# Probability transposes one step later, and one score matmul over both halves of k for a head's first query tile

## The chip, the cores and the metric

The kernel runs on one NeuronCore of a Trainium2 chip. The metric is the device time of one execution in microseconds (us). TensorE (PE) multiplies, VectorE (DVE) and ScalarE (ACT) do elementwise work and reductions, GpSimd (POOL) does slower elementwise work, SyncE (SP) issues the DMAs. Each engine runs its own queue of instructions in order, and engines wait for one another by semaphores.

## The reference

Four sequences of 512 tokens, width 1024, go through attention with 16 heads of 64 and then through a mixture of low-rank experts. What matters here is the attention:

```python
q = apply_rotary(norm(x) @ Wq)          # also k; v without rotary
logits = einsum('bhqd,bhkd->bhqk', q, k)
logits = where(causal, logits, -1e9) / sqrt(64)
attn = softmax(logits)
out = einsum('bhqk,bhkd->bhqd', attn, v) @ Wo
x = x + norm(out)
x = x + norm(expert_mixture(norm(x)))
```

## The kernel before

Every float32 operand of a matmul is split into a high part in a format that TensorE takes at full rate (`fp32r`) and a low part, the remainder. A projection is three products, high by high, low by high and high by low.

**Units and slots.** The attention is cut into 32 units. Unit u is one pair of heads of one sequence. A slot is the program stretch in which unit u is projected; it has 8 steps, s = 0 to 7. `slot(pair, b, half, ahead)` is written out for each engine, and `run_slots` calls it in the same order for all: some slots are written out, most lie in loops of two slots, b = 0 and b = 1. Slot number u is odd where b is 1. In the slots with `ahead` (u = 2 to 9) a further tile of x is normalised, transposed and stored for the second half. `closing` slots 32 and 33 have no projection.

**The eight score tiles.** A unit has 2 heads with 4 query tiles of 128 each, so q = 0 to 7; tile i = q % 4 of a head sees 128 x (i + 1) keys because of the causal mask. Because `trailing(u, s, 1)` shifts by one step, tile q of unit u - 1 is worked on in step s = q + 1 of slot u (q = 7 in step 0 of slot u + 1). For each tile:

- TensorE, `scores`: two matmuls into the score bank, stationary q_hl (the rows of one head's q high, the other 64 rows its low part), moving k_hh (k high in both halves of the partitions) and then k_lo (k low in the head's own half, zeros in the other). Both have 128 x (i + 1) columns and add into the same columns.
- VectorE, `negate` (L1053): adds the causal mask to the scores, scales by a negative factor and takes the running minimum, which gives prob (not yet exponentiated) and nmax.
- ScalarE, `exponent` (L740): the exponential with its sum.
- VectorE, `invert` (L1063): the reciprocal of the sum.
- GpSimd, `divide` (L595): prob times that reciprocal.
- TensorE, `turn_probs` (L1499), two steps later: `trailing(u, s, 3)`: i + 1 transposes of 128x128 into a pT bank.
- ScalarE, `pt_high` (L751), copies the high part out, then VectorE, `pt_low` (L1071), subtracts it for the low part. Both are in the step of the transposes.

**The rest of a slot.** `project` is 72 matmuls of 512 columns, 9 per step in three thirds; the scores stand behind the first third, the transposes behind the second. `attend` (L1517 to L1520) multiplies the transposed probabilities by v: head 0 at s = 0, head 1 at s = 4, of unit u - 2. Its result has two halves: ScalarE's `o_lower` (L784) copies the lower half out (s = 1 and s = 5) and VectorE's `o_add` (L1105) adds it to the upper half (s = 1 and s = 6, between `negate` and `invert`). VectorE has `rotate` (L1080, the rotary product, s = 3 and 6, also between `negate` and `invert`), `q_low` (L1085, s = 4 and 5, after `pt_low`), `v_low` (L1096, s = 2), and `k_low` (L1091 and L1092, a subtraction that gives k_lo and a copy within k_hh; head 0 at s = 7 after `pt_low`, head 1 at s = 0 of the next slot). ScalarE has `v_raw` (s = 0), `v_high` (s = 2), `q_high` (s = 3), `k_high` (s = 6). The first scores of a unit wait for `k_low` of head 0.

**Weights.** For each pair of slots, in the slots with b = 1, GpSimd's `w_pairs` (L606, L607) stands at s = 2 and 5 and `w_low` (L613) at s = 4 and 7, behind that step's `divide`, and ScalarE's `w_high` (L733) at s = 4 and 6. The third weight's `w_high` and `w_low` are in the slot with b = 0 at s = 0 and s = 1.

Each engine's order is the order in which its `slot` is written: for ScalarE `exponent`, `v_raw` or `o_lower`, `v_high`, `pt_high`, the others; for VectorE `negate`, `rotate`, `o_add`, `invert`, `v_low`, `pt_low`, the others. With `ahead`, `k_low` of head 0 stands before `invert`, and VectorE also has statistics (L990, L991, L996) at s = 4 and their scale at s = 6.

After the units come sixteen token tiles of output projection and experts, which the change doesn't touch.

Of the kernel before, what the change touches and what calls it, by code (L numbers as in the profile page):

```python
# [19 lines left out]
F32R = mybir.dt.float32r  # L20
# [43 lines left out]
HOLD_AT = (4, 7)  # L64
X_BANKS = (4, 5, 6, 7, 2, 3)


def sandwich_kernel(nc, x, wqkv, wo, ar, bt, br, cos, sin, scratch, out):
    with ExitStack() as ctx:
# [3 lines left out]
        def sem(name):  # L73
            return ctx.enter_context(nc.semaphore(name))
# [64 lines left out]
        k_hh = sb(sB, "k_hh", [P, 2, 2, SEQ], F32R)  # L139
        k_lo = sb(sB, "k_lo", [P, 2, 2, SEQ], F32R)  # L140
# [14 lines left out]
        o_sum = sb(sB, "o_sum", [DH, 2, SEQ])  # L155

# [67 lines left out]
        neg_done = sem("neg_done")  # L224
        exp_done = sem("exp_done")
# [470 lines left out]
        def _(act):  # L696
# [47 lines left out]
            def pt_high(u, s):  # L744
                a, q, g = trailing(u, s, 3)
                if real(a):
                    i, h = q % QT, q // QT
                    act.wait_ge(t_done, g + 1)
                    if late(a, 1):
                        act.wait_ge(pv_done, 2 * a + h - 1)  # L750
                    act.activation(pT_hi[:, h, 0:i + 1, P * i:P * i + P],  # L751
                                   pt_ps[q % 2][:, 0:P * (i + 1)].rearrange("p (j t) -> p j t", j=i + 1),
                                   ACT.Copy).then_inc(pt_hi_done, 1)
# [46 lines left out]
            def slot(pair, b, half, ahead=False):  # L800
# [6 lines left out]
                for s in range(STEPS):  # L807
# [3 lines left out]
                    if s == 1 and real(u - 2):  # L811
                        o_lower(u - 2, 0)
                    if s == 5 and real(u - 2) and not (isinstance(u, int) and u > UNITS):
                        o_lower(u - 2, 1)
# [173 lines left out]
        def _(dve):  # L988
# [56 lines left out]
            def negate(u, s):  # L1045
                a, q, g = trailing(u, s, 1)
                if real(a):
                    n = P * (q % QT + 1)
                    dve.wait_ge(s_done, g + 1)
                    if late(g, 4):  # L1050
                        dve.wait_ge(t_done, g - 3)
                    dve.sem_inc(gate_dve, 1)
                    dve.tensor_tensor_reduce(prob[:, q % 4, 0:n], sc_ps[q % 2][:, 0:n], mask[:, SEQ - n:SEQ],  # L1053
                                             -SOFT, 3e38, ALU.add, ALU.min, nmax[:, q % 4:q % 4 + 1]
                                             ).then_inc(neg_done, 1)
# [9 lines left out]
            def pt_low(u, s):  # L1065
                a, q, g = trailing(u, s, 3)
# [57 lines left out]
            def slot(pair, b, half, ahead=False):  # L1124
# [4 lines left out]
                for s in range(STEPS):  # L1129
# [7 lines left out]
                    if s == 1 and real(u - 2) and not closing:  # L1137
                        o_add(u - 2, 0)
                    if s == 6 and real(u - 2) and not (closing and u > UNITS):
                        o_add(u - 2, 1)  # L1140
# [11 lines left out]
                    if closing and s == 1 and real(u - 2):  # L1152
                        o_add(u - 2, 0)
                    if real(u):
                        if s in (4, 5):
                            q_low(u, b, s - 4)
                        if s == 7 and not leads:
                            k_low(u, b, 0)
# [240 lines left out]
        def _(pe):  # L1399
# [76 lines left out]
            def scores(u, s, b):  # L1476
                a, q, g = trailing(u, s, 1)
                if real(a):
# [5 lines left out]
                    if late(g, 2):  # L1484
                        pe.wait_ge(neg_done, g - 1)
                    qc, kc = slice(P * i, P * i + P), slice(0, P * i + P)
                    products(sc_ps[q % 2][:, kc], [(q_hl[:, ab, h, qc], k_hh[:, ab, h, kc]),
                                                   (q_hl[:, ab, h, qc], k_lo[:, ab, h, kc])], True, True
                             ).then_inc(s_done, 1)

            def turn_probs(u, s):
                a, q, g = trailing(u, s, 3)
# [58 lines left out]
            def slot(pair, b, half, ahead=False):  # L1551
                u = 2 * pair + b + UPH * half
                n = pair + PAIRS * half
                for s in range(STEPS):
# [13 lines left out]
                    if s == 0:  # L1568
                        attend(u - 2, b, 0)
                    if s == (3 if isinstance(u, int) and u == UNITS + 1 else 4):  # L1570
                        attend(u - 2, b, 1)
# [191 lines left out]
```

## Time and profile before

| | |
|---|---|
| median of 3 runs | 1069.91 us (1069.79 to 1070.48) |
| the profiled execution | 1069.58 us |
| its span, first to last instruction | 1067.8 us |
| TensorE busy | 1049.9 us |
| VectorE, ScalarE, GpSimd busy | 756.9, 591.3, 439.4 us |
| mean granted TensorE clock | 0.998 |
| attention units | to about 820 us |

The profile is one execution. TensorE's matmuls overlap in its pipeline, so its busy time says that something was always in flight, not that no start was late; late starts are read from the distances between starts. An idle time with a releaser tells which instruction of which engine ended it. A row's second number is the duration; the distance between two starts is the cost in a queue.

### The profile page before, as it was taken

Reading aid. Unit: us, or ns where it says so; the run is one execution under the profiler, and the core shown is the slowest. Engines: PE = TensorE matmul, PEld = TensorE weight load, DVE = VectorE, ACT = ScalarE, POOL = GpSimd, SP = SyncE. Lnnn points to the kernel's source line nnn. Section 1 sums busy time; section 2 is a strip of 40 time slices with the busy share of each in tenths; the row PEclk is TensorE's granted clock in tenths of the full one; section 3 lists DMA queues with packets and bytes.
Section 4 is the critical chain, followed back from the end, with each engine's and each line's share of the span. In section 5 each row is a group of like instructions: output and inputs, shape, how many; then the busy total and the mean of one; then the engine's idle time right before and its main releaser. Section 6 shows DMA issues by size and latency. Waiting matters only on the chain.

```text
span 1067.8 us, 20069 instructions
## 1 busy us (share of the span) xinstructions
PE 1049.9 (98%) x5559; PEld 871.3 (82%) x5559; DVE 756.9 (71%) x2138; ACT 591.3 (55%) x1390; POOL 439.4 (41%) x422
## 2 busy tenths in 40 slices
PE   7999999999999999999999999999999999999996
PEld 6888888888888888888888888888877888888884
DVE  8777777776666666666666666666766877777777
ACT  7556666666555665565555655555576333333334
POOL 4153443435353635444452625344457232333221
PEclk9999999999999999999999999999999999999999
DMA  7022324241311256021111112020333323322311
GB/s 280 36 84 70 128 69 128 74 129 55 104 51 34 95 182 227 10 71 33 52 49 31 52 29 69 10 69 17 87 132 93 108 88 107 118 99 87 109 61 60
DMA packets 58663, 90.36 MB, mean 85 GB/s; under 512 B 3568, under 2 KB 36336, under 8 KB 58608
## 3 DMA queue, kind: packets, MB, share of 16 engines
q1 hardware_dynamic: 58464, 89.44, 25.9%
q8 instruction: 25, 0.41, 0.2%
q14 instruction: 30, 0.25, 0.1%
q10 hardware_dynamic: 144, 0.26, 0.1%
HBM read 64.52 MB, written 25.17 MB: 84 GB/s over the span
## 4 chain that ended last, share of the span: by engine, by line
PE 90%; DVE 3%; issue 2%; ACT 2%; POOL 0%; DVEq 0%; ACTq 0%; POOLq 0%
PE bank L1472 46%; PE bank L1403 25%; PE bank L1499 6%; PE bank L1518 3%; PE bank L1517 3%; PE bank L1633 2%; PE bank L1610 1%; PE bank L1445 1%; PE bank L1634 1%; PE bank L1520 1%; PE bank L1433 1%; ACT prob L740 1%; DVE prob L1053 0%; DVE k_hh L1092 0%; PE bank L1415 0%
## 5 line engine op out<-in xcount | busy, mean ns | idle before, releaser
L595 POOL TENSOR_SCALAR prob<-prob,rinv 128x128 f32<-128x128 f32 (+3 forms) x256 | 150.5, 588 | 436.8 <-DVE rinv L1063 436.8
L1472 PE MATMUL bank<-big_hi,w_hi 128*128 128x512 f32 (+1 forms) x776 | 329.4, 424 | 0.3 <-DVE big_lo L1034 0.3
L740 ACT ACTIVATE prob<-prob,nmax 128x128 f32<-128x128 f32 (+3 forms) x256 | 144.0, 562 | 304.3 <-DVE nmax L1053 302.7
L1472 PE MATMUL bank<-big_hi,w_lo 128*128 128x512 f32 (+1 forms) x776 | 304.5, 392 | 0.0
L1472 PE MATMUL bank<-big_lo,w_hi 128*128 128x512 f32 (+1 forms) x776 | 302.1, 389 | 0.0
L1472 PEld LDWEIGHTS bank<-big_hi,w_lo 128*128 128x128 f32 x776 | 145.6, 188 | 33.2
L1071 DVE TENSOR_TENSOR pT_lo<-bank,pT_hi 128x128 fp32r<-128x128 f32 (+3 forms) x256 | 123.7, 483 | 56.0 <-ACT pT_hi L751 53.3
L1472 PEld LDWEIGHTS bank<-big_hi,w_hi 128*128 128x128 f32 x776 | 146.6, 189 | 16.5 <-issue 0.4
L1472 PEld LDWEIGHTS bank<-big_lo,w_hi 128*128 128x128 f32 x776 | 147.1, 190 | 11.6
L1063 DVE RECIPROCAL rinv<-rsum 128x1 f32<-128x1 f32 x256 | 40.8, 159 | 129.3 <-ACT prob L740 128.9
L1053 DVE CUSTOM_DVE_ANT_0 prob<-bank,mask 128x128 f32<-128x128 f32 (+3 forms) x256 | 124.1, 485 | 9.2 <-PE bank L1403 5.1
L1499 PE MATMUL bank<-ident,prob 128*128 128x128 f32 x640 | 112.0, 273 | 1.5 <-POOL prob L595 1.0
L751 ACT ACTIVATE pT_hi<-bank 128x128 fp32r<-128x128 f32 (+3 forms) x256 | 108.8, 425 | 2.1 <-PE bank L1499 0.5
L1499 PEld LDWEIGHTS bank<-ident,prob 128*128 128x128 f32 x640 | 82.9, 141 | 32.5 <-POOL prob L595 6.0
L674 POOL TENSOR_TENSOR res<-res,x 128x1024 f32<-128x1024 f32 x14 | 33.4, 2389 | 146.1 <-ACT res L705 146.1
L613 POOL TENSOR_TENSOR w_lo<-w_sum,w_hi 128x1024 fp32r<-128x1024 f32 x32 | 83.0, 2593 | 8.0 <-ACT w_hi L733 7.7
L1403 PE MATMUL bank<-k_lo,q_hl 128*128 128x128 f32 (+3 forms) x256 | 82.2, 321 | 0.0
L1403 PE MATMUL bank<-k_hh,q_hl 128*128 128x128 f32 (+3 forms) x256 | 80.7, 315 | 0.5 <-DVE k_hh L1092 0.5
L1403 PE MATMUL bank<-big_hi,w_hi 128*128 128x512 f32 x192 | 79.5, 414 | 0.0
L1403 PE MATMUL bank<-big_lo,w_hi 128*128 128x512 f32 x192 | 75.2, 391 | 0.0
L1403 PE MATMUL bank<-big_hi,w_lo 128*128 128x512 f32 x192 | 75.0, 391 | 0.0
L1105 DVE TENSOR_TENSOR o_sum<-bank,o_low 64x512 f32<-64x512 f32 x64 | 43.3, 677 | 37.5 <-ACT o_low L784 37.5
(146 smaller groups left out, 1927.7 us busy)
## 6 DMA issues: line engine op xcount, KB each, us to landing
w_raw<-in_wqkv SPq DMA_DIRECT2D x48, 512.0 KB, 4.4
attention_out<-o_sum SPq DMA_DIRECT2D x64, 128.0 KB, 2.3
w_raw<-attention_out SPq DMA_DIRECT2D x16, 512.0 KB, 4.8
land<-in_x SPq DMA_DIRECT2D x16, 512.0 KB, 3.7
out<-res SPq DMA_DIRECT2D x14, 512.0 KB, 2.6
xin<-in_x SPq DMA_DIRECT2D x12, 512.0 KB, 5.7
xT_hold_hi<-xin SPq DMA_DIRECT2D x8, 512.0 KB, 3.6
xT_hold_lo<-xn SPq DMA_DIRECT2D x8, 512.0 KB, 5.4
```

The source lines that it names most:

```text
L595: pool.tensor_scalar(p, p, rinv[:, q % 4:q % 4 + 1], 1.0, ALU.mult, ALU.mult).then_inc(prob_done, 1)
L613: pool.tensor_tensor(w_lo[:, m, :], src, w_hi[:, m, :].bitcast(F32), ALU.subtract).then_inc(w_lo_done[m], 1)
L674: pool.tensor_tensor(res[:, i, :], res[:, i, :], x1[:, i, :], ALU.add).then_inc(res_done, 1)
L740: act.activation(prob[:, q % 4, 0:n], prob[:, q % 4, 0:n], ACT.Exp, scale=-1.0, bias=nmax[:, q % 4:q % 4 + 1], accum_out=rsum[:, q % 4:q % ...
L751: act.activation(pT_hi[:, h, 0:i + 1, P * i:P * i + P], pt_ps[q % 2][:, 0:P * (i + 1)].rearrange("p (j t) -> p j t", j=i + 1), ACT.Copy).t ...
L1053: dve.tensor_tensor_reduce(prob[:, q % 4, 0:n], sc_ps[q % 2][:, 0:n], mask[:, SEQ - n:SEQ], -SOFT, 3e38, ALU.add, ALU.min, nmax[:, q % 4:q ...
L1063: dve.reciprocal(rinv[:, q % 4:q % 4 + 1], rsum[:, q % 4:q % 4 + 1]).then_inc(inv_done, 1)
L1071: dve.tensor_tensor(pT_lo[at], pt_ps[q % 2][:, 0:P * (i + 1)].rearrange("p (j t) -> p j t", j=i + 1), pT_hi[at].bitcast(F32), ALU.subtract ...
L1105: dve.tensor_tensor(o_sum[:, h, :], o_ps[0:DH, :], o_low[:, :], ALU.add).then_inc(osum_done, 1)
L1403: mm = pe.matmul(dst, lhsT, rhs, start=first and n == 0, stop=last and n == len(terms) - 1)
L1472: done = pe.matmul(grp_ps[(b + k) % 2][:, cols], w, xt[:, cols], start=at == 0, stop=at == GROUP_MM - 1)
L1499: last = pe.transpose(pt_ps[q % 2][:, P * j:P * j + P], prob[:, q % 4, P * j:P * j + P], ident[:, :])
```

## The change

`TURN_LAG = 4` takes the place of the 3 in `turn_probs`, `pt_high` and `pt_low`: transposes and what follows them come one step later (for step s the tile is now q = s - 4 modulo 8 instead of s - 3). `attend` moves from s = 0 and 4 to s = 1 and 5 (in the last slot from 3 to 4), `o_lower` from s = 1 and 5 to 2 and 6, and `o_add` from s = 1 and 6 to s = 2 and 6, where it now stands behind `pt_low` and not before `invert`.

For a head's first query tile (i = 0) the two score matmuls of 128 columns become one of 256: k_hh and k_lo are now the halves of one tensor k_all, the moving operand is [2 x 128] columns of it, and the two products lie side by side in the score bank. VectorE adds the second to the mask first, waits for that, and uses the result in place of the mask.

```diff
+TURN_LAG = 4
-        k_hh = sb(sB, "k_hh", [P, 2, 2, SEQ], F32R)
-        k_lo = sb(sB, "k_lo", [P, 2, 2, SEQ], F32R)
+        k_all = sb(sB, "k_all", [P, 2, 2, 2, SEQ], F32R)
+        k_hh, k_lo = k_all[:, 0, :, :, :], k_all[:, 1, :, :, :]
...
             def pt_high(u, s):
-                a, q, g = trailing(u, s, 3)
+                a, q, g = trailing(u, s, TURN_LAG)
...
-                    if s == 1 and real(u - 2):
+                    if s == 2 and real(u - 2):
                         o_lower(u - 2, 0)
-                    if s == 5 and real(u - 2) and not (isinstance(u, int) and u > UNITS):
+                    if s == 6 and real(u - 2) and not (isinstance(u, int) and u > UNITS):
                         o_lower(u - 2, 1)
...
+                    added = mask[:, SEQ - n:SEQ]
+                    if q % QT == 0:
+                        added = low_masked[:, :]
+                        dve.tensor_tensor(added, sc_ps[0][:, P:2 * P], mask[:, SEQ - P:SEQ], ALU.add).then_inc(low_added, 1)
+                        dve.wait_ge(low_added, 2 * a + q // QT + 1)
+                        dve.sem_inc(gate_dve, 1)
-                    dve.tensor_tensor_reduce(prob[:, q % 4, 0:n], sc_ps[q % 2][:, 0:n], mask[:, SEQ - n:SEQ],
+                    dve.tensor_tensor_reduce(prob[:, q % 4, 0:n], sc_ps[q % 2][:, 0:n], added,
...
             def pt_low(u, s):
-                a, q, g = trailing(u, s, 3)
+                a, q, g = trailing(u, s, TURN_LAG)
...
-                    if s == 1 and real(u - 2) and not closing:
-                        o_add(u - 2, 0)
-                    if s == 6 and real(u - 2) and not (closing and u > UNITS):
-                        o_add(u - 2, 1)
...
-                    if closing and s == 1 and real(u - 2):
+                    if s == 2 and real(u - 2):
                         o_add(u - 2, 0)
+                    if s == 6 and real(u - 2) and not (closing and u > UNITS):
+                        o_add(u - 2, 1)
...
+                    if i == 0:
+                        pe.matmul(sc_ps[0][:, 0:2 * P].rearrange("p (a n) -> p a n", a=2), q_hl[:, ab, h, qc],
+                                  k_all[:, :, ab, h, kc], start=True, stop=True).then_inc(s_done, 1)
...
             def turn_probs(u, s):
-                a, q, g = trailing(u, s, 3)
+                a, q, g = trailing(u, s, TURN_LAG)
...
-                    if s == 0:
+                    if s == 1:
                         attend(u - 2, b, 0)
-                    if s == (3 if isinstance(u, int) and u == UNITS + 1 else 4):
+                    if s == (4 if isinstance(u, int) and u == UNITS + 1 else 5):
                         attend(u - 2, b, 1)
```

## Rows read from the trace of the kernel before

**Rows 1.** The page: engine, busy us, share of the span, number of instructions.
```profile
PE 1049.9 (98%) x5559; PEld 871.3 (82%) x5559; DVE 756.9 (71%) x2138; ACT 591.3 (55%) x1390; POOL 439.4 (41%) x422
```

**Rows 2.** TensorE's waits, whole span: line, releaser, us in total, times, longest.
```profile
PEld bank L1499 <- POOL prob L595: 6.0, 12, 1.4
...
PE bank L1403 <- DVE k_hh L1092: 0.5, 1, 0.5
```

**Rows 3.** Waits of VectorE and of ScalarE between 100 and 780 us.
```profile
DVE rinv L1063 <- ACT prob L740: 112.5, 154, 1.7
...
DVE prob L1053 <- PE bank L1403: 0.2, 1, 0.2
...
ACT prob L740 <- DVE nmax L1053: 267.5, 169, 4.7
```

**Rows 4.** VectorE's timeline, negations of two slots: start us, duration us, engine, line.
```profile
583.51 0.29 DVE L1053 CUSTOM_DVE_ANT_0 prob<-bank,mask 128x128 f32<-128x128 f32 x1
...
608.53 0.29 DVE L1053 CUSTOM_DVE_ANT_0 prob<-bank,mask 128x128 f32<-128x128 f32 x1
...
611.24 0.41 DVE L1053 CUSTOM_DVE_ANT_0 prob<-bank,mask 128x256 f32<-128x256 f32 x1
...
614.01 0.55 DVE L1053 CUSTOM_DVE_ANT_0 prob<-bank,mask 128x384 f32<-128x384 f32 x1
...
615.78 0.69 DVE L1053 CUSTOM_DVE_ANT_0 prob<-bank,mask 128x512 f32<-128x512 f32 x1
...
622.46 0.42 DVE L1053 CUSTOM_DVE_ANT_0 prob<-bank,mask 128x256 f32<-128x256 f32 x1
...
624.67 0.54 DVE L1053 CUSTOM_DVE_ANT_0 prob<-bank,mask 128x384 f32<-128x384 f32 x1
...
627.81 0.69 DVE L1053 CUSTOM_DVE_ANT_0 prob<-bank,mask 128x512 f32<-128x512 f32 x1
...
631.76 0.29 DVE L1053 CUSTOM_DVE_ANT_0 prob<-bank,mask 128x128 f32<-128x128 f32 x1
```

**Rows 5.** TensorE's timeline around a first-tile and a second-tile score pair.
```profile
508.65 0.22 PE L1403 MATMUL bank<-k_hh,q_hl 128*128 128x128 f32 x1
...
509.34 0.40 PE L1472 MATMUL bank<-big_hi,w_lo 128*128 128x512 f32 x1
...
511.85 0.28 PE L1403 MATMUL bank<-k_lo,q_hl 128*128 128x256 f32 x1
...
512.43 0.39 PE L1472 MATMUL bank<-big_hi,w_lo 128*128 128x512 f32 x1
```

**Rows 6.** Instructions by line and form: busy us, mean ns, idle before.
```profile
L1071 DVE TENSOR_TENSOR pT_lo<-bank,pT_hi 128x512 fp32r<-128x512 f32 x64 | 43.2, 676 | 3.1 <-ACT pT_hi L751 3.1
...
L1071 DVE TENSOR_TENSOR pT_lo<-bank,pT_hi 128x128 fp32r<-128x128 f32 x64 | 18.6, 290 | 0.0
...
L751 ACT ACTIVATE pT_hi<-bank 128x512 fp32r<-128x512 f32 x64 | 37.3, 584 | 0.5 <-PE bank L1499 0.5
...
L751 ACT ACTIVATE pT_hi<-bank 128x128 fp32r<-128x128 f32 x64 | 16.4, 257 | 0.0
```

**Rows 7.** VectorE's timeline: an instruction that waits for the one before it.
```profile
152.69 0.21 DVE L996 BATCH_NORM_AGGREGATE mv<-stats 128x2 f32<-128x12 f32 x1 [0.15 <-DVE stats L991]
```

**Rows 8.** ScalarE's timeline: the o_low copy.
```profile
620.01 0.60 ACT L784 ACTIVATE o_low<-bank 64x512 f32<-64x512 f32 x1
```

**Rows 9.** Timelines of VectorE and GpSimd around 312 us.
```profile
311.28 0.87 DVE L1091 TENSOR_TENSOR k_lo<-rot,k_hh 64x512 fp32r<-64x512 f32 x1 [0.16 <-issue]
312.17 2.57 DVE L1092 CAST k_hh<-k_hh 64x512 fp32r<-64x512 f32 x1
...
311.58 2.87 POOL L613 TENSOR_TENSOR w_lo<-w_sum,w_hi 128x1024 fp32r<-128x1024 f32 x1
```

**Rows 10.** VectorE's timeline: first negation of unit 1 and of unit 8.
```profile
67.61 0.29 DVE L1053 CUSTOM_DVE_ANT_0 prob<-bank,mask 128x128 f32<-128x128 f32 x1
...
244.39 0.29 DVE L1053 CUSTOM_DVE_ANT_0 prob<-bank,mask 128x128 f32<-128x128 f32 x1
```

More of the change, by code:

```diff
@@ L155, in sandwich_kernel @@
         o_sum = sb(sB, "o_sum", [DH, 2, SEQ])
+        low_masked = sb(sB, "low_masked", [P, P])
         hold_hi = xin[:, 1, :].rearrange("p (c t) -> p c t", c=KC)
@@ L224, in sandwich_kernel @@
         neg_done = sem("neg_done")
+        low_added = sem("low_added")
         exp_done = sem("exp_done")
@@ L1486, in scores @@
                     qc, kc = slice(P * i, P * i + P), slice(0, P * i + P)
-                    products(sc_ps[q % 2][:, kc], [(q_hl[:, ab, h, qc], k_hh[:, ab, h, kc]),
-                                                   (q_hl[:, ab, h, qc], k_lo[:, ab, h, kc])], True, True
-                             ).then_inc(s_done, 1)
+                    if i == 0:
+                        pe.matmul(sc_ps[0][:, 0:2 * P].rearrange("p (a n) -> p a n", a=2), q_hl[:, ab, h, qc],
+                                  k_all[:, :, ab, h, kc], start=True, stop=True).then_inc(s_done, 1)
+                    else:
+                        products(sc_ps[q % 2][:, kc], [(q_hl[:, ab, h, qc], k_hh[:, ab, h, kc]),
+                                                       (q_hl[:, ab, h, qc], k_lo[:, ab, h, kc])], True, True
+                                 ).then_inc(s_done, 1)
             def turn_probs(u, s):
-                a, q, g = trailing(u, s, 3)
+                a, q, g = trailing(u, s, TURN_LAG)
                 if real(a):
```

## Prediction

> **What bounds the kernel now.** I read the busy shares first. TensorE is busy 98% of the span and VectorE 71% [rows 1]. That page invites the sum "TensorE work removed is time removed". So I read next what TensorE waits for: its weight loads for the probability transposes stood 6.0 us behind GpSimd's division in the whole span, 12 times, 1.4 us at most [rows 2]. Almost nothing is lost on TensorE.
>
> Then I asked whether the others have room, from the waits of VectorE and ScalarE between 100 and 780 us, where the attention units run. VectorE waited 112.5 us for ScalarE's exponential, ScalarE 267.5 us for VectorE's negation, and VectorE only once, for 0.2 us, for scores of TensorE [rows 3]. So these two engines wait for each other and not for TensorE: they are a loop of their own. Its period is in VectorE's timeline. The first negation of a unit (128x128) starts at 583.51, 608.53 and 631.76 us [rows 4]: 25.02 us for a unit in an odd slot, 23.23 in an even one, 48.25 for the pair, 24.13 per unit. In the steady part I find these lengths repeated to 0.02 us in most units, which a queue fed by TensorE wouldn't do. TensorE's own stream has a period of 24.16. The kernel has two chains of one length, and only one looks busy. This is the main reading: whatever lengthens the VectorE-ScalarE loop by more than a few hundredths of a us per unit appears in the time.
>
> The eight intervals between negations in the even slot are 2.71, 2.77, 1.77 for the tiles q = 0, 1, 2, then 6.68 for q = 3 and 4 together, 2.21, 3.14 and 3.95 for q = 5, 6, 7 [rows 4].
>
> **TensorE's part.** From the start of a first-tile score pair to the start of the third matmul behind it are 0.69 us (508.65 to 509.34); from a single 256-column score matmul to the same place 0.58 (511.85 to 512.43) [rows 5]. The change turns the first into the second: 0.11 x 64 heads = 7.0 us off TensorE, about 0.22 per unit, period 23.94. If the two-part operand streamed badly, the nearest bound on the other side is the pair as it is, 0; neither end matters while the other loop is longer. The later transposes give the division one more step, some 3 us, so the waits of [rows 2] go; what they cost TensorE's own timeline I take as at most 1.4. At the end of attention the last transposes are now directly in front of the last `attend`, with no matmuls between: the 512-column ScalarE copy and VectorE subtraction, 0.58 + 0.68 us [rows 6], with hand-over some 1.4, become a wait there. These two cancel.
>
> **The added VectorE instruction.** The low-part addition is 128x128 from PSUM and SBUF, the form and size of the negation, 0.29 us [rows 4]. The negation has to wait for it on its own engine with a gate increment between, as the statistics' aggregation does: 0.15 us idle [rows 7]. 0.45 per head, 0.9 per unit. Queued behind it are the negation, so ScalarE's exponential, and everything behind both. Bounds: 0.29 (wait free) to 0.6 (wait twice as long). The 29% idle of VectorE doesn't hide it, since that idle is its waiting inside the loop.
>
> **What moves inside the loop.** Each interval is reworked from the one of before (even slot, which is free of weight work), following which of the two engines comes last.
> q = 0: the o_low copy (0.60 us [rows 8]) and the o_sum addition leave it. What remains is the bare pattern of q = 2 (1.77), 0.5 less for a third as many columns in negation and exponential, 0.2 more for a 256- instead of a 128-column turn: 1.48. Plus 0.45: 1.93 against 2.71, -0.78.
> q = 1: o_low now stands before v_high on ScalarE (+0.60 and its issue), o_sum behind pT_lo on VectorE (+0.61), and the turn has 384 columns, not 512 (-0.13): 3.97 against 2.77, +1.20.
> q = 2: its turn was 128 columns and is 512: +0.33 on ScalarE and +0.39 on VectorE [rows 6], less 0.06 that the reciprocal hides: 2.42, +0.65.
> q = 3 and 4: o_low leaves (-0.7), narrower turns (-0.5), the addition comes (+0.45): 5.95 against 6.68, -0.73.
> q = 5: before, o_sum ran while ScalarE worked and cost nothing. Now o_low delays the copy pT_hi by 0.6, and o_sum (0.6) stands behind pT_lo; the turn is 384 instead of 512 columns (-0.2): 3.29, +1.08.
> q = 6: turn of 512 instead of 128 columns in front of k_low, +0.71, less 0.2 for a division that no longer meets k_low: 3.64, +0.50.
> q = 7: 128 columns instead of 256: 3.65, -0.30.
> Sum 24.85 against 23.23: **+1.62 us in an even slot**. So the order costs 0.7 to 0.8 beside the addition's 0.9: the two o_low/o_sum steps no longer stand where the other engine's work covered them, and the wide turns now meet the steps in which VectorE has rotate and k_low.
>
> **The odd slot** has the weight work. The same differences give 25.02 + 1.62 = 26.64, less 0.7 because the second q_low now loses less to GpSimd's weight sums, less 0.1 at q = 6: 25.8, +0.8. But k_low comes 0.71 later. In this profile k_lo starts at 311.28 and GpSimd's w_lo (128x1024) at 311.58, and the copy k_hh then took 2.57 us instead of 0.42, ending 0.29 after w_lo [rows 9]: VectorE's SBUF-only copy stood still for GpSimd's instruction. It happened fully once, at 312 us, because k_lo is usually just ahead. With k_lo 0.71 later, w_lo is in front by about 0.4 in every odd slot: k_lo then waits for the rest of w_lo, some 2.0 us, less what the division's meeting cost: 27.4, **+2.4 us in an odd slot**. The Trainium skill (SBUF — State Buffer, Who interferes with whom) says that a VectorE instruction with two SBUF inputs, or in a two-port mode, contends with GpSimd, and that whoever issues first holds the pair for the whole instruction. By that rule the wait is the rest of w_lo, as this row shows; if the port were shared by halves, the odd slot would cost some 1 us less. The same section says that an instruction with one SBUF input doesn't contend, so by it the new addition is free of this.
>
> **The sum.** Steady units 9 to 29, 11 even and 10 odd: 11 x 1.62 + 10 x 2.40 = 41.8, less 2.2 for the one meeting already paid at 312 us: 39.6. Units 1 to 7, in which later x tiles are prepared as well, took 244.39 - 67.61 = 176.8 us [rows 10]; the same differences apply, save that q = 3 is held by statistics and division (0 instead of -0.17) and that k_low there precedes the turn (no lock): 188.8, +12.0. Unit 8 +1.5, unit 0 +0.7. The last two units and the closing slots, which have o_low and o_sum too: +3, bounds 0 to 6. TensorE's slack before the scores of each unit (under 1 us) is used up once: -0.8. Together +56.0. The profiled execution took 1069.6 us (span 1067.8), 0.3 below the median of the runs: 1069.6 + 56.0 = 1125.6, and I forecast 1125. The part behind 830 us isn't touched. On TensorE's 7.0 us nothing is gained: it waits at the first scores of a unit for k_low.
>
> **Rivals.**
> (1) The order costs what I say, but w_lo and k_lo don't meet, because GpSimd or ScalarE falls into another phase: odd slots 25.8 instead of 27.4, so 10 x 1.6 = 16 less, 1109. For it: the meeting needs 0.4 us of phase. Against: GpSimd starts w_lo at a fixed distance from the reciprocal.
> (2) **Faster**: VectorE's and ScalarE's idle absorbs the additions, and TensorE's stream sets the period. Place: the unit loop; price: -7.0 and -1.4 of lost waits, +1.4 at the end: 1062.6. It decides if the loop's pair period stays below 2 x 23.94 = 47.9 us. For it: 29% idle VectorE. Against: the period is 48.25 already, with no wait for TensorE in [rows 3].
> (3) The loop lengthens by the additions only, since moving o_low and o_sum off q = 0 and q = 4 repays itself: 0.9 x 30 = 27, less the slack of 0.8: 1096.
> (4) Worse: more VectorE copies meet GpSimd, or TensorE's granted clock falls behind waits of 2 to 4 us per pair of units (it is 0.998 over the span now): above 1138.
> (5) The merged matmul isn't cheaper at all. It would change nothing while (2) is false, and is counted in the forecast.
>
> **How the numbers follow.** Forecast 0.58, covering 1115 to 1136 through the bounds of the addition and of the closing slots; (1) 0.22, 1100 to 1115; (3) 0.07, 1085 to 1100; (2) 0.07; (4) 0.05; 0.01 for no change. The range that holds 8 in 10 with part of (3) is 1092 to 1138. About 0.2% is what a measurement of this kernel can tell from no change: faster 0.07, same 0.02, slower 0.91.
>
> **What would show it.** In the changed profile: the eight intervals (1.93, 3.97, 2.42, 5.95, 3.29, 3.64, 3.65) from VectorE's timeline; pair period 52.3; q = 6 interval near 6.0 in odd slots with a k_lo of 2 us or more; TensorE waiting for k_hh at the first scores of a unit, some 30 times, where it is now once, for 0.5 us [rows 2]; no more wait for the division; VectorE still with no wait for TensorE. It would be wrong if VectorE showed waits for scores in the steady part, or if the pair period were below 48.

## The result, and the profile after

The changed kernel takes **1144.53 us** (median of 4 runs, 1143.57 to 1145.21) against 1069.99 (1069.79 to 1070.48): ratio 1.0695, 95% interval 1.0677 to 1.0714. The profiled execution took 1143.57 us, span 1141.7. So it is slower, as forecast, but by 74 us where 56 were forecast, and above the range's upper end of 1138.

The page of the changed kernel, busy us of each engine and the granted TensorE clock in tenths over 40 slices:

```profile
PE 1074.2 (94%) x5495; PEld 878.2 (77%) x5495; DVE 790.3 (69%) x2202; ACT 591.2 (52%) x1390; POOL 428.4 (38%) x422
...
PEclk9999999999999899999898999999899999999999
```

TensorE has 64 instructions fewer than in [rows 1] and yet 24.3 us more busy time. No removed matmul can explain that; the row of clocks shows TensorE working at a lower clock for a part of the time: four slices fall to 8, and the mean over the span is 0.975 where it was 0.998.

Waits between 100 and 840 us of the changed kernel (line, releaser, us in total, times, longest):

```profile
ACT prob L743 <- DVE nmax L1062: 329.3, 210, 4.6
DVE rinv L1072 <- ACT prob L743: 118.9, 182, 1.2
PE bank L1495 <- DVE k_all L1101: 41.0, 17, 3.6
...
DVE prob L1062 <- PE bank L1410: 12.2, 10, 2.0
DVE prob L1062 <- DVE low_masked L1059: 11.1, 55, 0.6
```

Against [rows 2, 3]: TensorE now waits 41.0 us for the copy k_hh, 17 times, up to 3.6 us at a time, where it waited 0.5 once. VectorE waits for ScalarE and ScalarE for VectorE still, and longer. The last two lines are the added wait behind the low-part addition, and one that I had said would not appear: VectorE waiting ten times, up to 2.0 us, for a score matmul.

**One odd slot of the changed kernel**, negations in VectorE's timeline (start us, duration us), with what ended an idle time in brackets, and the first two of the even slot behind it:

```profile
630.67 0.29 DVE L1062 CUSTOM_DVE_ANT_0 prob<-bank,low_masked 128x128 f32<-128x128 f32 x1 [0.19 <-DVE low_masked L1059]
632.14 0.42 DVE L1062 CUSTOM_DVE_ANT_0 prob<-bank,mask 128x256 f32<-128x256 f32 x1
634.49 0.69 DVE L1105 TENSOR_TENSOR v_hl<-bank,v_hl 128x512 fp32r<-128x512 f32 x1 [1.08 <-ACT v_hl L779]
...
636.16 0.54 DVE L1062 CUSTOM_DVE_ANT_0 prob<-bank,mask 128x384 f32<-128x384 f32 x1
638.58 0.68 DVE L1062 CUSTOM_DVE_ANT_0 prob<-bank,mask 128x512 f32<-128x512 f32 x1
...
642.26 0.29 DVE L1062 CUSTOM_DVE_ANT_0 prob<-bank,low_masked 128x128 f32<-128x128 f32 x1 [0.19 <-DVE low_masked L1059]
644.61 0.42 DVE L1062 CUSTOM_DVE_ANT_0 prob<-bank,mask 128x256 f32<-128x256 f32 x1
...
647.92 0.54 DVE L1062 CUSTOM_DVE_ANT_0 prob<-bank,mask 128x384 f32<-128x384 f32 x1
...
653.97 0.69 DVE L1062 CUSTOM_DVE_ANT_0 prob<-bank,mask 128x512 f32<-128x512 f32 x1
...
658.17 0.29 DVE L1062 CUSTOM_DVE_ANT_0 prob<-bank,low_masked 128x128 f32<-128x128 f32 x1 [0.19 <-DVE low_masked L1059]
661.72 0.42 DVE L1062 CUSTOM_DVE_ANT_0 prob<-bank,mask 128x256 f32<-128x256 f32 x1 [1.99 <-PE bank L1410]
```

The slot lasts 658.17 - 630.67 = 27.50 us. Its intervals are 1.47, 4.02, 2.42, then 3.68 + 2.35 = 6.03, 3.31, 6.05, 4.20. The prediction counted the addition and its wait (0.48 from start to start) with q = 0, here they lie at the end of q = 7; counted as there: 1.95, 4.02, 2.42, 6.03, 3.31, 6.05, 3.72 against 1.93, 3.97, 2.42, 5.95, 3.29, near 6.0, 3.65. **The reworked intervals held to 0.1 us.** Only the last line doesn't fit: q = 0 of the even slot took 3.55 instead of 1.47, and VectorE waited 1.99 of them for scores.

**What happens there** is in the slot two units earlier, at 596 us: GpSimd's w_lo and VectorE's k_lo and k_hh of the changed kernel,

```profile
596.14 2.34 POOL L616 TENSOR_TENSOR w_lo<-w_sum,w_hi 128x1024 fp32r<-128x1024 f32 x1
...
596.31 2.71 DVE L1100 TENSOR_TENSOR k_all<-rot,k_all 64x512 fp32r<-64x512 f32 x1
599.03 0.42 DVE L1101 CAST k_all<-k_all 64x512 fp32r<-64x512 f32 x1
...
602.04 0.69 DVE L1100 TENSOR_TENSOR k_all<-rot,k_all 64x512 fp32r<-64x512 f32 x1
```

TensorE's timeline behind it,

```profile
599.59 0.57 PE L1495 MATMUL bank<-k_all,q_hl 128*128 128x256 f32 x1 [3.29 <-DVE k_all L1101]
599.96 0.63 PE L1479 MATMUL bank<-big_hi,w_hi 128*128 128x512 f32 x1
600.39 0.63 PE L1479 MATMUL bank<-big_lo,w_hi 128*128 128x512 f32 x1
...
606.73 0.39 PE L1479 MATMUL bank<-big_hi,w_hi 128*128 128x512 f32 x1
606.96 0.40 PE L1479 MATMUL bank<-big_lo,w_hi 128*128 128x512 f32 x1
```

and TensorE in stretches of 3 us (stretch, its length, busy us and instructions, granted clock, DMA share, GB/s):

```profile
596.00:599.00 3.00, 0.30 (x2) 0.98 0.84 337
599.00:602.00 3.00, 2.41 (x7) 0.50 0.01 3
602.00:605.00 3.00, 3.00 (x11) 0.50 0.00 0
605.00:608.00 3.00, 3.00 (x19) 0.89 0.00 0
608.00:611.00 3.00, 3.00 (x17) 1.00 0.00 0
```

k_lo starts 0.17 us behind w_lo and takes 2.71 instead of 0.69, ending 0.54 after w_lo. TensorE stands still for 3.29 us until k_hh is there. Then its granted clock is 0.50, the 1.2 GHz level, over two stretches, although from 602 on it works without a gap; 512-column matmuls start 0.43 us apart (599.96, 600.39) instead of 0.23 (606.73, 606.96). In those six microseconds 18 matmul records stand where the next six have 36. So the scores of q = 1 come late, and VectorE and ScalarE, which set the time, wait for them.

**The account** goes by the first negation of a unit in the changed kernel (units 1, 8, 9 and 30; unit 0 starts at 42.85, and in the kernel before units 0, 9 and 30 at 42.35, 269.06 and 777.13):

```profile
70.20 0.29 DVE L1062 CUSTOM_DVE_ANT_0 prob<-bank,low_masked 128x128 f32<-128x128 f32 x1 [0.19 <-DVE low_masked L1059]
...
256.73 0.29 DVE L1062 CUSTOM_DVE_ANT_0 prob<-bank,low_masked 128x128 f32<-128x128 f32 x1 [0.19 <-DVE low_masked L1059]
...
282.57 0.29 DVE L1062 CUSTOM_DVE_ANT_0 prob<-bank,low_masked 128x128 f32<-128x128 f32 x1 [0.56 <-DVE low_masked L1059]
...
845.76 0.29 DVE L1062 CUSTOM_DVE_ANT_0 prob<-bank,low_masked 128x128 f32<-128x128 f32 x1 [0.19 <-DVE low_masked L1059]
```

| stretch | before, us | after, us | measured | forecast |
|---|---|---|---|---|
| to the first negation | 42.35 | 42.85 | +0.5 | 0 |
| unit 0 | 25.26 | 27.35 | +2.1 | +0.7 |
| units 1 to 7 | 176.78 | 186.53 | +9.8 | +12.0 |
| unit 8 | 24.67 | 25.84 | +1.2 | +1.5 |
| units 9 to 29 | 508.07 | 563.19 | +55.1 | +39.6 |
| unit 30 and all behind it | 290.67 | 295.94 | +5.3 | +3.0 |
| TensorE's slack | | | | -0.8 |
| span | 1067.8 | 1141.7 | +73.9 | +56.0 |

The clock's part can be read here. Of the +55.1, the lengthened q = 0 of the even slots is 13.0: it is 1.47 where nothing disturbs it, and in the ten even slots from unit 11 to 29 it took 2.15, 3.32, 1.92, 2.28, 3.40, 3.50, 3.55, 2.05, 2.28 and 3.28. The other 42.1 is the order, the additions and the meeting of k_lo with w_lo. Unit 1, in the stretch before, lost 0.8 in the same way (q = 0 is 2.28 there, and 1.47 in e3 below).

### The profile page after: what moved, and what is told of

Its sections match the earlier page's. It is cut to its first block, busy times and chain, and to the rows that moved or that the text cites. A ratio compares the mean times of both kernels' runs of the same rounds, so it can differ in the third digit from the quotient of the medians.

```text
span 1141.7 us, 20114 instructions
## 1 busy us (share of the span) xinstructions
PE 1074.2 (94%) x5495; PEld 878.2 (77%) x5495; DVE 790.3 (69%) x2202; ACT 591.2 (52%) x1390; POOL 428.4 (38%) x422
## 4 chain that ended last, share of the span: by engine, by line
PE 60%; issue 14%; DVE 11%; ACT 10%; DVEq 1%; ACTq 1%; POOL 0%; POOLq 0%
PE bank L1479 26%; PE bank L1410 19%; PE bank L1510 4%; ACT pT_hi L754 3%; PE bank L1529 3%; ACT prob L743 3%; DVE prob L1062 2%; PE bank L1528 2%; ACT o_low L787 2%; PE bank L1644 2%; DVE k_all L1100 1%; PE bank L1621 1%; PE bank L1495 1%; PE bank L1452 1%; ACT k_all L769 1%
## 5 line engine op out<-in xcount | busy, mean ns | idle before, releaser
L1479 PE MATMUL bank<-big_hi,w_lo 128*128 128x512 f32 (+1 forms) x776 | 308.4, 397 | 0.0
L1479 PE MATMUL bank<-big_lo,w_hi 128*128 128x512 f32 (+1 forms) x776 | 307.4, 396 | 0.0
L1479 PEld LDWEIGHTS bank<-big_hi,w_lo 128*128 128x128 f32 x776 | 148.6, 191 | 34.5
L1479 PEld LDWEIGHTS bank<-big_hi,w_hi 128*128 128x128 f32 x776 | 149.7, 193 | 17.4 <-issue 0.6
L1479 PEld LDWEIGHTS bank<-big_lo,w_hi 128*128 128x128 f32 x776 | 150.4, 194 | 11.5
L1062 DVE CUSTOM_DVE_ANT_0 prob<-bank,mask 128x256 f32<-128x256 f32 (+2 forms) x192 | 105.7, 551 | 17.4 <-PE bank L1410 15.2
L1410 PE MATMUL bank<-k_all,q_hl 128*128 128x256 f32 (+2 forms) x384 | 99.9, 341 | 0.0
L616 POOL TENSOR_TENSOR w_lo<-w_sum,w_hi 128x1024 fp32r<-128x1024 f32 x32 | 79.0, 2470 | 6.7 <-ACT w_hi L736 6.0
L1410 PEld LDWEIGHTS bank<-k_all,q_hl 128*128 128x128 f32 x384 | 69.7, 188 | 13.8
L1529 PE MATMUL bank<-pT_lo,v_hl 128*64 128x512 f32 (+3 forms) x256 | 67.0, 329 | 0.0
```

The lines of the kernel that those rows point to most:

```text
L616: pool.tensor_tensor(w_lo[:, m, :], src, w_hi[:, m, :].bitcast(F32), ALU.subtract).then_inc(w_lo_done[m], 1)
L1410: mm = pe.matmul(dst, lhsT, rhs, start=first and n == 0, stop=last and n == len(terms) - 1)
L1479: done = pe.matmul(grp_ps[(b + k) % 2][:, cols], w, xt[:, cols], start=at == 0, stop=at == GROUP_MM - 1)
L1529: pe.matmul(o_ps[0:DH, cols], v_hl[:, b, j, h, 0:DH], pT_lo[:, h, j, cols], start=False, stop=False)
```

## The experiments

The theory: VectorE and ScalarE in turn set the time; the additions, the order of the later steps and the meeting of k_lo with w_lo lengthen their loop; and the wait of TensorE behind that meeting drops its clock. Each part is taken alone, then mended.

**e2: the merged matmul and the addition alone**, everything else where it was.

```
 AHEAD = EARLY // 2
-TURN_LAG = 4
+TURN_LAG = 3
...
-                    if s == 2 and real(u - 2):
+                    if s == 1 and real(u - 2):
                         o_lower(u - 2, 0)
...
-                    if s == 1:
+                    if s == 0:
                         attend(u - 2, b, 0)
```

(o_add, the second o_lower and the second attend go back to their steps of before in the same way.)

> The merged score matmul with the addition on VectorE, but transposes, attend, o_lower and o_add where they were before. Loop theory: intervals of before plus 0.45 at q = 0 and q = 4, pair period 48.25 + 1.8 = 50.05 us, 1.75 over TensorE's 48.3: 10.5 pairs x 1.75 = 18, the units with x tiles 7 x 0.9 = 6, the last ones 1 to 2: 1095 us, q = 6 in odd slots near 4.0 (k_lo still ahead of GpSimd's w_lo), and no cut of TensorE's clock. Rival (VectorE's idle hides the addition and TensorE's 7 us are gained): 1063.

Measured: 1095.66 us (1095.53 to 1096.04), ratio 1.0242 (1.0225 to 1.026). Its waits between 100 and 840 us, and the first negation of three successive units:

```profile
PE bank L1512 <- POOL prob L598: 9.1, 22, 1.7
```

```profile
602.40 0.29 DVE L1062 CUSTOM_DVE_ANT_0 prob<-bank,low_masked 128x128 f32<-128x128 f32 x1 [0.19 <-DVE low_masked L1059]
...
627.90 0.29 DVE L1062 CUSTOM_DVE_ANT_0 prob<-bank,low_masked 128x128 f32<-128x128 f32 x1 [0.19 <-DVE low_masked L1059]
...
652.10 0.29 DVE L1062 CUSTOM_DVE_ANT_0 prob<-bank,low_masked 128x128 f32<-128x128 f32 x1 [0.19 <-DVE low_masked L1059]
```

The pair of units lasts 49.70 us instead of 48.25 [rows 4]. 64 matmuls fewer, and 25.8 us more, of 64 x 0.48 = 30.7 us added on VectorE. The idle 29% of VectorE hides none of it in an even slot, which takes 24.20 us instead of 23.23. An odd slot takes 25.50 instead of 25.02: there the q = 4 interval falls from 4.20 to 3.71 with its addition in place at q = 3, since the second q_low, now later, takes 1.10 us beside GpSimd's weight sums instead of 1.58. TensorE isn't what sets the time; its shorter work shows as new waits for GpSimd's division. This settles the main reading against rival (2). Over the whole kernel the new addition costs 0.40 per head (25.8 / 64).

**e1: the order alone**, without the merged matmul and the addition.

```
-                    if q % QT == 0:
-                        added = low_masked[:, :]
-                        dve.tensor_tensor(added, sc_ps[0][:, P:2 * P], mask[:, SEQ - P:SEQ], ALU.add).then_inc(low_added, 1)
-                        dve.wait_ge(low_added, 2 * a + q // QT + 1)
-                        dve.sem_inc(gate_dve, 1)
...
-                    if i == 0:
-                        pe.matmul(sc_ps[0][:, 0:2 * P].rearrange("p (a n) -> p a n", a=2), q_hl[:, ab, h, qc],
-                                  k_all[:, :, ab, h, kc], start=True, stop=True).then_inc(s_done, 1)
-                    else:
...
```

> The later transposes with the moved attend, o_lower and o_add, but the scores of a first query tile as before: two matmuls, no addition on VectorE. The loop theory (VectorE and ScalarE are a loop of their own that sets the time of a unit): against the changed kernel each unit loses two additions of 0.45 us, so 0.9, in all about 28 of its 1144.5 us, and some more where TensorE's wait becomes short enough that its clock isn't cut: 1101 to 1116 us, with intervals between negations as in the changed kernel (4.02, 2.42, 3.68 to the next, and so on), and q = 6 in odd slots still near 6.0. The rival, that the added instruction is the whole loss and the new order costs nothing, gives the time of before, 1070, or a little less.

Measured: 1110.54 us (1107.76 to 1111.44), ratio 1.0375 (1.0358 to 1.0392). The q = 6 interval of odd slots is 6.06 to 6.13, so the meeting with w_lo comes from the order and needs no addition. TensorE's waits for k_hh are shorter than in the changed kernel:

```profile
PE bank L1405 <- DVE k_all L1096: 26.5, 13, 2.9
```

2.9 us at most, not 3.6, and the mean granted clock is 0.992: the drop shows in a few slots only (q = 0 took 2.89 at unit 1, 4.09 at unit 11 and 2.72 at unit 13, else 1.5 to 1.7). e1 and e2 together give 40.6 + 25.8 = 66.4 of the 74.5 that the whole change costs; the other 8 us come only with both. The clock can account for them: the three long intervals of e1 hold 5.3 us of excess, those of the changed kernel 13.8 (both with unit 1).

**e3: the changed kernel without the meeting.** GpSimd holds back the second w_lo until k_lo and k_hh of the slot are done.

```
                         if s in (4, 7):
+                            if s == 7:
+                                pool.wait_ge(qk_lo_done, 4 * u + 3)
                             w_low(s // 7, n + 1)
```

> The changed kernel, but GpSimd starts the w_low of step 7 only once k_low of head 0 is done. If w_lo holds up k_lo in each odd slot and the wait of TensorE that comes of it (up to 3.6 us) cuts its clock, both go: q = 6 in odd slots from 6.05 to 3.9 to 4.4, the interval at q = 0 in even slots from 1.47 to 3.55 back to 1.47 everywhere, granted clock near 1.0: about 18 + 12 to 15 off, 1110 to 1115 us. If the meeting isn't the cause, the time stays at 1144. If it is, but the clock has another cause, 1126.

Measured: 1110.75 us (1110.35 to 1111.36), ratio 1.0384 (1.0367 to 1.0402), 34 us below the changed kernel. Its k_lo of both heads and its w_lo in an odd slot, TensorE's waits for k_hh, and the span with the clock:

```profile
630.18 0.67 DVE L1102 TENSOR_TENSOR k_all<-rot,k_all 64x512 fp32r<-64x512 f32 x1
630.87 0.42 DVE L1103 CAST k_all<-k_all 64x512 fp32r<-64x512 f32 x1
...
633.88 1.12 DVE L1102 TENSOR_TENSOR k_all<-rot,k_all 64x512 fp32r<-64x512 f32 x1
```

```profile
631.37 2.42 POOL L616 TENSOR_TENSOR w_lo<-w_sum,w_hi 128x1024 fp32r<-128x1024 f32 x1 [1.33 <-DVE k_all L1103]
```

```profile
PE bank L1497 <- DVE k_all L1103: 31.7, 27, 1.6
```

```profile
core 0: 1108.6 us, clock 0.999
```

k_lo of head 0 takes 0.67 again, the q = 6 interval of odd slots is 4.01, q = 0 is 1.47 in every unit from 1 to 30, and VectorE has no wait for scores. w_lo waits 1.33 us, and this isn't quite free: it moves the division behind it, and k_lo of head 1 (at 633.88) then takes 1.12 us where an even slot's takes 0.69, so the q = 7 interval of odd slots is 4.63 instead of 4.20. The wait of TensorE is still there 27 times, but 1.6 us at most, and the clock stays at its upper level. So one cause, the meeting, brings both the longer odd slot and the lost clock: about 20 us and 14 us, as the next run divides them.

**e4: the clock by itself.** The meeting stays; TensorE is kept at work in front of the first scores of an even slot by 12 matmuls into a bank that the scores overwrite.

```
+                    if s == 1 and b == 0 and real(u) and not ahead and not (isinstance(u, int) and u == 0):
+                        pe.wait_ge(neg_done, STEPS * (u - 1) - 1)
+                        for _ in range(12):
+                            pe.matmul(sc_ps[0][:, :], w_hi[:, 0, 0:P], xT_hi[:, b, 0, :], start=True, stop=True)
                     scores(u, s, b)
```

> The changed kernel with 12 more matmuls of 512 columns on TensorE ahead of the first scores of a unit in even slots (from unit 9 on), where it waits for k_hh up to 3.6 us; their results are overwritten by the scores. They take 12 x 0.23 = 2.8 us of that wait. If the cut clock is what stretches q = 0 in even slots (1.47 to 3.55), it stays at 1.5 to 2.0 there, the granted clock is near 1.0 and VectorE no longer waits for scores, while q = 6 in odd slots stays 6.05: about 10 to 14 us less, 1131 to 1135. If the stretch has another cause (a transfer, the order of transposes), the time stays at 1144 or grows.

Measured: 1130.84 us (1130.52 to 1131.79), ratio 1.0572 (1.0554 to 1.0589): **13.7 us less although TensorE does more**. TensorE around the added matmuls, and the stretches behind them:

```profile
643.66 2.90 PE L1578 MATMUL bank<-big_hi,w_hi 128*128 128x512 f32 x12
647.12 0.39 PE L1495 MATMUL bank<-k_all,q_hl 128*128 128x256 f32 x1 [0.56 <-DVE k_all L1101]
```

```profile
645.00:648.00 3.00, 2.44 (x11) 1.00 0.42 172
648.00:651.00 3.00, 3.00 (x19) 1.00 0.00 0
```

The scores still start when k_hh is there, so the meeting is untouched (q = 6 of odd slots 6.15, 0.1 more than without the added matmuls), but the granted clock is 1.00 behind it, the scores of q = 1 are in time, and q = 0 of even slots is 1.47. The 13.7 us agree with the 13.0 read from the intervals. What remains of e3's gain, 1130.84 - 1110.75 = 20.1, is found in the same intervals: the ten odd slots from unit 10 on are longer by 17.7 in all (27.58 against 25.87 in most), unit 0 by 1.6 (27.34 against 25.72), where k_lo meets w_lo too, and unit 1 by 0.8, where nothing was added and the clock fell.

**e10: the order alone, without the meeting** (e1 with e3's line).

> The order of the changed kernel alone: no merged scores and no addition, and GpSimd's w_low of step 7 waits for k_low, so that neither the port nor TensorE's clock plays a part. If additions and order add up in one loop, it takes e3_port's 1110.8 less 0.97 us for each of 31 units: 1080.7. That is 11 us over the kernel before, for nothing but the places of o_low, o_sum and the wide turns. If the order costs nothing by itself, 1069.

Measured: 1086.24 us (1085.99 to 1086.69), ratio 1.0157 (1.0141 to 1.0172): the pure order costs 16.7 us. I had expected 5.5 us less. The miss is the q = 4 interval of odd slots: from 604.17 to 607.00 it takes 2.83 us where e3 has 2.34. VectorE and GpSimd in it:

```profile
605.76 1.22 DVE L1091 TENSOR_TENSOR q_hl<-rot,q_hl 64x512 fp32r<-64x512 f32 x1
```

```profile
603.71 2.72 POOL L616 TENSOR_TENSOR w_lo<-w_sum,w_hi 128x1024 fp32r<-128x1024 f32 x1
```

Between the two negations stands the second q_low, with 1.22 us instead of 0.73: it starts while GpSimd's first w_lo of the slot still runs (to 606.43). In e3 the added instruction puts q_low later (623.24), and w_lo ends at 623.42. The weight sums, which q_low met in the kernel before, start only at 607.18 here. That the overlap is the cause is read from these rows; no run moved that w_lo. e3's additions on top of this order cost 24.5 us.

**e5: o_add where ScalarE's work covers it**, on top of e3: in front of the reciprocal, at steps 3 and 7 instead of 2 and 6, while the exponential runs.

```
+                    if s in (3, 7) and real(u - 2) and not (closing and u > UNITS):
+                        o_add(u - 2, s // 7)
...
-                    if s == 2 and real(u - 2):
+                    if s == 2 and real(u - 2) and closing and u > UNITS:
                         o_add(u - 2, 0)
-                    if s == 6 and real(u - 2) and not (closing and u > UNITS):
-                        o_add(u - 2, 1)
```

> The kernel of e3_port, with the two o_sum additions on VectorE at steps 3 and 7 ahead of the reciprocal, where VectorE otherwise waits for ScalarE's exponential. Theory (what the order costs is work that stands behind the subtraction and so is no longer covered): 0.6 us less at q = 1 (4.01 to 3.4) in all units and at q = 5 (3.31 to 2.7), nothing added at q = 2 and q = 6; in odd slots the 0.6 of q = 5 comes back at q = 6, since ScalarE's weight copy holds the exponential there. 31 x 0.6 + 11 x 0.5 + 7 x 0.6 = 28 off 1110.8: 1082. Rival (an addition costs its time wherever it stands): 1111.

Measured: 1085.67 us (1084.82 to 1086.38), ratio 1.0148 (1.0131 to 1.0165), 25.1 below e3. The intervals of q = 1 and q = 5 fall from 4.01 to 3.42 and from 3.31 to 2.72, each by one addition of 0.6. The q = 6 of odd slots takes one of them back (4.60 instead of 4.01), and that of even slots 0.1; the others stay: the pair falls from 50.81 to 49.21. I had expected 1082, 3.7 less: in units 1 to 7 the q = 6 interval grows from 3.03 to 3.50, so the second 0.6 is for the most part not gained there. The same instruction on the same engine costs nothing at q = 2 and up to 0.6 elsewhere, by its place.

**e6: the first o_lower behind pT_hi on ScalarE**, on top of e5.

```
-                    if s == 2 and real(u - 2):
-                        o_lower(u - 2, 0)
...
                     pt_high(u, s)
+                    if s == 2 and real(u - 2):
+                        o_lower(u - 2, 0)
```

> As e5_o_add, with ScalarE's first o_low copy behind pT_hi at step 2, so that v_high is no longer held up: another 0.6 us off q = 1 (3.4 to 2.8), 31 times. The loop's pair period would be 47.9 us, just that of TensorE with the merged matmuls (48.3 - 0.4), so the time ends between 1064 and 1068, in part bound by either. If there is anything else in the loop, 1070 and more.

Measured: **1065.94 us** (1065.82 to 1066.32), ratio 0.9967 (0.9955 to 0.998). The interval of q = 1 falls from 3.42 to 2.66 (q = 2 grows from 2.42 to 2.56): v_high no longer stands behind o_lower on ScalarE, and so the v_low step of VectorE waits 0.32 us for it instead of 1.08 (the changed kernel's row at 634.49). The pair of units is now 47.92 us. With its steps placed anew and GpSimd's w_lo held back, the change is on the fast side of the kernel before, with both additions per unit still in it.

**e7: the second w_high one step later**, on top of e6, to take the weight copy on ScalarE off the odd slot's step 6.

```
                         if b == 1 and not (isinstance(u, int) and u == UNITS - 1):
-                            if s == 6:
+                            if s == 7:
                                 w_high(1, n + 1)
```

> As e6_o_lower, with ScalarE's weight copy of step 6 behind pT_hi of step 7, so that the exponential of q = 6 isn't held up in odd slots: about 1 us per pair off the VectorE-ScalarE loop, pair period 46.9. Then TensorE sets the time, and the merged matmuls' 0.11 us per head are gained: 1069.9 - 7.0 and a little of the transposes' waits: 1062 to 1064. If TensorE still waits for k_hh in each unit, the loop is longer than I say.

Measured: 1066.30 us (1066.26 to 1066.66), ratio 0.997: nothing gained, a miss. A timeline of VectorE (the first negation of three units, and one wait between) and its waits for scores:

```profile
580.36 0.29 DVE L1064 CUSTOM_DVE_ANT_0 prob<-bank,low_masked 128x128 f32<-128x128 f32 x1 [0.19 <-DVE low_masked L1061]
...
587.74 0.69 DVE L1064 CUSTOM_DVE_ANT_0 prob<-bank,mask 128x512 f32<-128x512 f32 x1 [0.28 <-PE bank L1412]
...
604.82 0.29 DVE L1064 CUSTOM_DVE_ANT_0 prob<-bank,low_masked 128x128 f32<-128x128 f32 x1 [0.19 <-DVE low_masked L1061]
...
628.29 0.29 DVE L1064 CUSTOM_DVE_ANT_0 prob<-bank,low_masked 128x128 f32<-128x128 f32 x1 [0.19 <-DVE low_masked L1061]
```

```profile
DVE prob L1064 <- PE bank L1412: 2.6, 9, 0.3
```

The step did what it was meant to, q = 6 of the odd slot fell from 4.58 to 3.65, but q = 0 to 2 grew from 6.70 to 7.38 (580.36 to 587.74), and VectorE now waits for TensorE there. The pair stays at 47.93. 47.9 is twice the 23.94 that the prediction gave as TensorE's period with merged matmuls: the loop has become short enough that the other chain takes over.

**e8: e7 without the merged matmul and the addition** (edit as in e1).

> As e7_w_high, but the scores of a first query tile by two matmuls as before and no addition on VectorE. TensorE's stream is then that of before, with no waits for the transposes' division: 1068 to 1070. The difference to e7_w_high is what the merged matmul is worth once TensorE sets the time: 7 us by the distances of starts, 64 x 0.11. If the merged matmul gains nothing on TensorE, both are equal.

Measured: 1068.28 us (1067.69 to 1068.89), ratio 0.9986 (0.9977 to 0.9996). Between 100 and 840 us:

```profile
DVE prob L1059 <- PE bank L1407: 26.4, 64, 0.9
```

VectorE waits for scores 64 times: here TensorE sets the time, and the pair lasts 48.34 us (581.42 to 629.76). Against e7's 47.93 the merged matmul is worth 0.41 us per pair, 0.10 per head, where I took 0.11 from [rows 5]. But units 1 to 7, which prepare later x tiles too and where VectorE is the later one, take 174.3 us here and 177.7 in e7: there the addition costs 3.4. In all, e7 is ahead by 2.0 us and not by the 7 that I had expected.

**e9: e7, merged only from unit 9 on** (two score matmuls and no addition in the eight slots that prepare x tiles).

```
-                    if q % QT == 0:
+                    if q % QT == 0 and not ahead:
                         added = low_masked[:, :]
...
-                    if i == 0:
+                    if i == 0 and not ahead:
                         pe.matmul(sc_ps[0][:, 0:2 * P].rearrange("p (a n) -> p a n", a=2), q_hl[:, ab, h, qc],
```

> As e7_w_high, but in the eight slots that also prepare x tiles (units 1 to 8) the scores of a first query tile are two matmuls without an addition. e7 took 177.7 us for units 1 to 7 where e8_no_merge took 174.3, since VectorE and ScalarE set the time there, and in the steady part 47.93 us per pair against 48.33, since TensorE does. If each part has the bound that I read, this kernel has the shorter of both: 3.3 us less than e7's 1066.3, 1063. Rival (the merge gives or takes the same everywhere): 1066.

Measured: **1064.71 us** (1064.39 to 1064.79), against 1069.58 of the kernel before beside it: ratio 0.9953 (0.9939 to 0.9967). Units 1 to 7 take 174.3, the pair 47.93 (579.10 to 627.03). It is the fastest version here and beats both kernels, by 4.9 and by 80 us. It missed my 1063 by 1.7: units 8 to 10 take 73.5 us here and 71.7 in e7, so half of what units 1 to 7 gain is lost behind them; no run shows why. Of the 4.9 us, 1.4 come without any merged matmul (e8 against the kernel before beside it, 1068.28 and 1069.72).

## Why the prediction was right or wrong

**What bounds the kernel: right.** VectorE and ScalarE were a second chain as long as TensorE's. e2 shows it directly (less on TensorE, 25.8 us more), and e7 and e8 show the two chains change places at 47.9 and 48.3 us per pair.

**TensorE's part: right.** 0.10 per merged pair measured (e7 against e8), 0.11 taken. Nothing of it is gained in the changed kernel.

**The added instruction: right, small miss.** 0.29 + 0.19 of wait = 0.48, not 0.45: the aggregation's 0.15 [rows 7] was the wrong one by 0.04, 64 x 0.03 = 1.9 us in all.

**What moves inside the loop: right.** The seven interval values held to 0.1; the even slot where the clock didn't fall is 24.96 (24.85 forecast). e5 and e6 bear out the two causes named, o_sum behind pT_lo and o_low in front of v_high: moving them gives back 25.1 and 19.7 us, together more than the 16.7 that the order costs by itself (e10), as their new places are better than those of before too.

**The odd slot: right.** 27.50 against 27.4, through w_lo in front of k_lo. The Trainium skill (SBUF — State Buffer, Who interferes with whom) says that a VectorE instruction with two SBUF inputs contends with GpSimd's reads, and that whoever issued first holds the shared ports for its whole instruction. The trace agrees: 2.71 us for the k_lo that started 0.17 behind w_lo, 0.67 in e3 where w_lo is held back. Rival (1) falls, though w_lo was ahead by 0.17 us only, and not by the 0.4 forecast.

**The step that failed is rival (4)'s clock.** The prediction had the mechanism, "TensorE's granted clock falls behind waits of 2 to 4 us", and gave it 0.05 together with other mishaps, and no term in the sum. The prediction's own sign of being wrong, waits of VectorE for scores in the steady part, is there (12.2 us, ten times). It had itself forecast the cause: k_hh some 2.4 us later in every odd slot with TensorE waiting at the first scores. Those two sentences were never put together. The term is 13.7 us by e4 and 13.0 by the intervals (13.8 with unit 1, which e4 leaves as it was); it was put at 0. With it the sum would have been 1139, some 5 below what was measured. The forecast of some 30 waits for k_hh missed for the same reason: there are 17 between 100 and 840 us, and 27 in e3 and e4, where TensorE keeps its clock and comes early in the even slots too.

**The rest of the gap** (17.9 us in all, 13.0 of it the clock) is terms mis-sized: units 9 to 29 without the clock +42.1 instead of 39.6 (the 0.03 of the wait twice per unit, and up to 0.1 in intervals); unit 0 +2.1 instead of 0.7, as there too k_lo met GpSimd (its q = 6 interval is 6.03, before it was 3.43, in e3 3.98); the closing units +5.3 instead of 3, within my bounds of 0 to 6; +0.5 ahead of the first negation; -0.8 of slack that isn't seen. Against these, units 1 to 7 came 2.2 lower, the clock's 0.8 in unit 1 counted, and unit 8 0.3 lower.

**The range was too narrow** for the same reason: its upper end of 1138 had no room for a term that the profile of before could not price, since behind its first instruction it holds no wait of TensorE above 1.4 us [rows 2]. A cost that isn't in the trace needed an end of its own there.

## What to carry to other kernels

Two engines that wait for each other can be the bound while each looks busy 55 to 70%: look for a period in the timeline that repeats to some hundredths of a microsecond with no wait for the busiest engine, and price each added or moved instruction by its place in that loop; here the same 0.6 us addition cost from nothing to 0.6. When a forecast says that TensorE will wait some microseconds, price what its granted clock does behind the wait too. And before giving up a change whose cost is its order, try its steps one place further and hold back what collides with them: here that, and the merge left out where VectorE is the later engine, turned +7% into -0.5%.

## What the runs showed of the hardware

In the changed kernel TensorE waited 3.2 to 3.6 us for k_hh eleven times, in unit 1 and in the ten odd slots from unit 10 on. Each time its granted clock then stood at 0.50, the 1.2 GHz level, for 3 to 7 us; in the slot shown for 6 to 7, of which the last part was gapless work. Waits of up to 1.6 us, 27 of them, left it at 0.999 (e3). In e1 the clock fell at three of the eleven waits above 2 us, those of 3.37, 2.86 and 2.49 us, and not at the eight of 2.33 to 2.50 (mean 0.992); waits of 2.49 and 2.50 us ended differently, and what decides between them no run shows. Twelve matmuls whose result nobody needs, put into the wait, gave back 13.7 us (e4). I hadn't expected the fall to come in every such slot, nor that a loop off TensorE would pay for it.
